# Input rows normed in a layout laid by the host, with mean and deviation spread by one ones matmul a tile in place of eight transposes

## What is computed

```python
def _layernorm(x, axis=-1, eps=1e-05):
    m = jnp.mean(x, axis=axis, keepdims=True)
    v = jnp.var(x, axis=axis, keepdims=True)
    return (x - m) / jnp.sqrt(v + eps)
...
qh = proj(q, Wq, bq)      # q = _layernorm(x): 16 x 128 x 1024, Wq 1024 x 1024
kh = proj(k, Wk, bk)      # k = v = ctx
vh = proj(v, Wv, bv)
qh, kh, vh = (interfere(qh), interfere(kh), interfere(vh))
scores = jnp.einsum('bhqdm,bhkdm->bhqkm', qh, kh) / math.sqrt(dk)
weights = jax.nn.softmax(scores, axis=3)
out = jnp.einsum('bhqkm,bhkdm->bhqdm', weights, vh)
...
x = x + jnp.tanh(g_xattn[0]) * (out @ Wo.T + bo)
x = x + jnp.tanh(g_ffn[0]) * ffn(_layernorm(x))
```

## Time and profile before

| | us |
|---|---|
| three runs | 1361.57, 1362.17, 1358.88 |
| median | 1361.57 |
| the profiled execution: its time | 1363.43 |
| its span in the trace | 1361.1 |
| PE busy in it | 1343.0 (99%) |
| DVE, ACT, POOL busy | 701.5, 409.0, 566.2 |

### The profile page before, as it was taken

One profiled execution on the slowest core, in us unless ns is written; L12 is line 12 of the kernel. 1 busy time (PEld: TensorE's weight loads), 2 busy tenths in 40 slices (PEclk: granted clock), 3 DMA queues, 4 the chain that ended last, 5 costly groups with the idle time before them and its releaser, 6 DMA issues.

```text
span 1361.1 us, 22258 instructions
## 1 busy us (share of the span) xinstructions
PE 1343.0 (99%) x8352; PEld 1116.5 (82%) x8352; DVE 701.5 (52%) x1372; ACT 409.0 (30%) x743; POOL 566.2 (42%) x775
## 2 busy tenths in 40 slices
PE   9999999999999999989999999999999999999999
PEld 8888888888778888778888888888778888888887
DVE  5432433345654545567777777777875243243110
ACT  3312221111112222355555555555451120111100
POOL 0899999999700000445566565655500000000000
PEclk9999999999999999989999999999999999999999
DMA  7898737345347676998877887777442202211011
GB/s 240 247 322 213 193 75 201 139 155 186 124 151 179 163 184 152 261 294 226 229 229 233 229 233 222 220 220 219 173 170 109 78 27 83 78 62 62 32 42 52
DMA packets 188938, 228.16 MB, mean 168 GB/s; under 512 B 26528, under 2 KB 124960, under 8 KB 188832
## 3 DMA queue, kind: packets, MB, share of 16 engines
q1 hardware_dynamic: 162912, 188.46, 46.7%
q10 hardware_dynamic: 25920, 38.28, 9.4%
HBM read 141.74 MB, written 83.89 MB: 166 GB/s over the span
## 4 chain that ended last, share of the span: by engine, by line
PE 69%; POOL 24%; DMA 2%; issue 2%; DVE 1%; ACT 1%; ACTq 1%; SPq 0%; POOLq 0%; DVEq 0%
PE bank L160 13%; PE bank L162 13%; PE bank L161 13%; POOL mixed_part L785 10%; POOL mixed_sum L792 6%; PE bank L1453 5%; PE bank L1473 4%; PE bank L1434 4%; PE bank L1436 4%; PE bank L1488 4%; PE bank L1435 4%; POOL mixed_sum L785 3%; PE bank L349 2%; POOL value_in L792 2%; PE bank L1460 1%
## 5 line engine op out<-in xcount | busy, mean ns | idle before, releaser
L1639 DVE TRANSPOSE_TENSOR_REDUCE part<-bank 128x16 f32<-128x512 f32 x256 | 174.3, 692 | 3.4 <-PE bank L1453 0.8
L1585 ACT ACTIVATE probT<-bank 128x512 f32<-128x512 f32 x256 | 138.9, 595 | 92.8 <-PE bank L1473 89.4
L1434 PE MATMUL bank<-w_hi,oT_hi 128*128 128x512 f32 x256 | 109.3, 427 | 3.3 <-POOL oT_lo L1759 3.0
L1255 DVE SCALAR_TENSOR_TENSOR raw_d<-bank,gates,raw_d 128x512 f32<-128x512 f32 x32 | 24.0, 751 | 167.4 <-PE bank L162 167.4
L160 PE MATMUL bank<-place_b,place_a 128*128 128x512 f32 x256 | 102.2, 399 | 0.4 <-DVE place_c L153 0.4
L160 PE MATMUL bank<-place_a,w_hi 128*128 128x512 f32 x256 | 101.6, 397 | 1.0 <-DVE place_a L153 1.0
L161 PE MATMUL bank<-place_c,place_a 128*128 128x512 f32 x256 | 102.0, 399 | 0.0
L575 DVE SCALAR_TENSOR_TENSOR stage_lo<-bank,bias_mixed,stage_hi 128x512 fp32r<-128x512 f32 x46 | 34.4, 750 | 130.9 <-ACT stage_hi L577 130.9
L160 PE MATMUL bank<-w_hi,yT_hi 128*128 128x512 f32 x256 | 101.8, 398 | 0.0
L1436 PE MATMUL bank<-w_hi,oT_lo 128*128 128x512 f32 x256 | 101.7, 397 | 0.0
L1435 PE MATMUL bank<-w_lo,oT_hi 128*128 128x512 f32 x256 | 101.1, 395 | 0.0
(11 more groups left out here) (241 smaller groups left out, 3076.2 us busy)
## 6 DMA issues: line engine op xcount, KB each, us to landing
k_rows<-stage_hi SPq DMA_DIRECT2D x128, 128.0 KB, 2.6
v_pad<-v_out SPq DMA_DIRECT2D x32, 512.0 KB, 2.6
v_place<-v_pad ACTq DMA_DIRECT2D x64, 256.0 KB, 4.2
tin<-in_ctx_cols SPq DMA_DIRECT2D x26, 512.0 KB, 4.3
k_in<-k_rows SPq DMA_DIRECT2D x64, 192.0 KB, 3.1
q_in<-q_rows SPq DMA_DIRECT2D x128, 96.0 KB, 3.3
q_rows<-wq_own SPq DMA_DIRECT2D x78, 128.0 KB, 2.5
raw_d<-x_mid SPq DMA_DIRECT2D x17, 512.0 KB, 3.3
```

The costliest lines, as they stand in the source:

```text
L1434: pe.matmul(o_bank[out][:], hi[:, c, :], wo_hi[:, k, cols], start=(k == 0), stop=False)
L1585: act.activation(probT[o % NPT][:, i].rearrange("k a p q -> k (a p q)"), two_bank[i][:], ACT.Exp).then_inc(s_exp, 1)
L1639: dve.tensor_reduce(part[o % NS][:, :, 2 * i:2 * i + 2, :].rearrange("k a p b -> k a (p b)"), one_bank[i][:].rearrange("k (a b t) -> k a b ...
```

## The change

The host lays x a second time, as `x_cols`: for each batch, partition p holds column p of each 128-column chunk, all rows (that is x already transposed). Each x tile is loaded twice, as rows (for the statistics) and as columns. `x_norm` still computes mean and inverse deviation from the rows, but writes them as two diagonal 128x128 matrices in place of the normed rows. `x_spread`, a new job, multiplies a 128x128 matrix of ones with the two diagonals side by side (256 columns, plain fp32): every partition of the bank then holds the 128 means and the 128 inverse deviations. Its DVE part subtracts and multiplies the column tile by them, in place. `x_split` adds two jobs without PE work which split the column tile from SBUF. A tile takes three jobs in the line where it took two.

The order moves too. The norm of x tiles 0 to 3 goes from the DVE part of v(8,0) .. v(11,0) to that of v(7,1) .. v(10,1); the PE step of a tile goes from behind v(8,1) .. v(11,1) to between v(8,0) and v(8,1), .. v(11,0) and v(11,1). In the query stage both keep their places. Loads of Wo's rows into `raw1` and `raw2` start later, since the ones, the diagonals and column tiles lie there. The transposes of the second layer stay.

```diff
-                src = ctx_cols[n % NB] if n < CTX else x_t[(n - CTX) * P:(n - CTX + 1) * P, :]
+                src = ctx_cols[n % NB]
...
+            ones = raw[1][:, 0:P]
+            diagonals = [raw[1][:, (1 + 2 * i) * P:(3 + 2 * i) * P] for i in range(2)]
...
+            def load_row_tile(b):
+                slot = b % 2 if b >= GB else 0
...
+                    at = norm_at[b - 1 if b <= GB else b - 2]
+                def load(sp):
+                    if b in (0, GB + 1):
+                        sp.wait_ge(line.emptied, at)
+                    else:
+                        sp.wait_ge(norm.s_stat, b if b <= GB else b - 1)
+                    sp.dma_start(tin[slot], x_t[b * P:(b + 1) * P, :]).then_inc(s_xrow[slot], 16)
...
+            def load_col_tile(b):
+                slot = b % 2 if b < GB else 2 + b % 2
+                tile = (raw[2][:], tin[1], flat_out[0], flat_out[1])[slot]
...
+                    sp.dma_start(tile, x_cols[b]).then_inc(s_xcol[slot], 16)
...
             def x_norm(b, job):
-                n = CTX + b
-                job.dve_pre = norm.vector_steps(b, *load_input(n))
+                tile, landed = load_row_tile(b)
+                norm_at[b] = len(line.jobs)
+
+                def steps(dve):
+                    if b == 0:
+                        link(dve.memset(ones, 1.0))
+                    first_half, variance, inverse, _ = norm.vector_stages(b, tile, landed)
+                    first_half(dve)
+                    variance(dve)
+                    inverse(dve)
+                    link(dve.tensor_scalar(diagonals[b % 2][:, 0:P], ident[:], norm.mv[:, 0:1], None, ALU.mult))
+                    dve.tensor_scalar(diagonals[b % 2][:, P:2 * P], ident[:], norm.rstd[:, 0:1], None,
+                                      ALU.mult).then_inc(norm.s_done, 1)
+                job.dve_pre = steps
                 job.act_pre = norm.scalar_step(b)
-            def x_jobs(b):
-                hi, lo = x_place(b // GB)
-                t_end[CTX + b] = transpose_jobs(line, tin[b % 2], norm.done(b), hi[:, b % GB, :, :], lo[:, b % GB, :, :])
+            def x_spread(b):
+                tile, landed = load_col_tile(b)
+                columns = tile.rearrange("p (k t) -> p k t", t=P)
+                def normalise(bank):
+                    def over_chunks(part):
+                        return bank[:, part * P:(part + 1) * P].unsqueeze(1).to_broadcast([P, KC, P])
+                    link(nc.vector.tensor_tensor(columns, columns, over_chunks(0), ALU.subtract))
+                    return nc.vector.tensor_tensor(columns, columns, over_chunks(1), ALU.mult)
+                spread_end[b] = line.add(Job(
+                    lambda bank: nc.tensor.matmul(bank[:, 0:2 * P], ones, diagonals[b % 2], start=True, stop=True),
+                    normalise, pe_wait=norm.done(b), dve_wait=landed))
+                return tile
+            def x_split(b, tile):
...
+                    def free(act):
+                        if b < GB:
+                            line.wait_filled(act, v_end[VALUE_ORDER[NB - GB + b]])
+                        act.wait_ge(line.emptied, spread_end[b])
+                    t_end[CTX + b] = line.add(Job(
+                        None, lambda bank, lo=lo, hi=hi, cols=cols: split_lo(lo, tile[:, cols], hi),
+                        act=lambda bank, hi=hi, cols=cols: split_hi(hi, tile[:, cols]), act_wait=free))
...
                 v_job(b, 0)
-                if j >= NB - GB:
-                    x_norm(j - NB + GB, line.jobs[-1])
                 if 6 <= j < 6 + KC:
                     query_chunk(j - 6)
+                if j >= NB - GB:
+                    tile = x_spread(j - NB + GB)
                 v_job(b, 1)
+                if NB - GB - 1 <= j < NB - 1:
+                    x_norm(j - NB + GB + 1, line.jobs[-1])
...
-                            x_jobs((g + 1) * GB + (1, 3, 5, 6).index(c))
+                            b = (g + 1) * GB + (1, 3, 5, 6).index(c)
+                            x_split(b, x_spread(b))
```

More of the change, by code:

```diff
@@ L495, in load @@
                 def load(sp):
[L496 to L499, removed]
+                    sp.wait_ge(line.emptied, free)
                     sp.dma_start(tin[slot], src).then_inc(s_tin[slot], 16)
@@ new lines, in build @@
+            diagonals = [raw[1][:, (1 + 2 * i) * P:(3 + 2 * i) * P] for i in range(2)]
+            norm_at, spread_end = {}, {}
+            s_xrow = [sem(f"s_xrow{i}") for i in range(2)]
+            s_xcol = [sem(f"s_xcol{i}") for i in range(4)]
+            def load_row_tile(b):
+                slot = b % 2 if b >= GB else 0
+                use = sum(1 for o in range(b + 1) if (o % 2 if o >= GB else 0) == slot)
+                if b == 0:
+                    at = t_end[CTX - 2]
+                elif b == GB + 1:
+                    at = t_end[CTX + GB - 1]
+                else:
[3 more added lines that the diff above has]
+                        sp.wait_ge(line.emptied, at)
+                    else:
+                        sp.wait_ge(norm.s_stat, b if b <= GB else b - 1)
+                    sp.dma_start(tin[slot], x_t[b * P:(b + 1) * P, :]).then_inc(s_xrow[slot], 16)
+                plan.append((at - 0.5, load))
+                return tin[slot], lambda eng: eng.wait_ge(s_xrow[slot], 16 * use)
@@ new lines, in load_col_tile, with load @@
+            def load_col_tile(b):
+                slot = b % 2 if b < GB else 2 + b % 2
+                use = b // 2 + 1 if b < GB else (b - GB) // 2 + 1
+                tile = (raw[2][:], tin[1], flat_out[0], flat_out[1])[slot]
+                if b in (GB, GB + 1):
+                    at = norm_at[b]
+                elif b == 0:
+                    at = wq_end[4]
+                elif b == 1:
+                    at = t_end[CTX - 1]
+                else:
+                    at = t_end[CTX + b - 2]
+                def load(sp):
+                    if b in (GB, GB + 1):
+                        sp.wait_ge(s_vst[b % 2], 16 * NB)
+                    else:
+                        sp.wait_ge(line.emptied, at)
+                    sp.dma_start(tile, x_cols[b]).then_inc(s_xcol[slot], 16)
+                plan.append((at - 0.4, load))
+                return tile, lambda eng: eng.wait_ge(s_xcol[slot], 16 * use)
@@ new lines, in x_split @@
+            def x_split(b, tile):
+                to_hi, to_lo = x_place(b // GB)
+                for half in range(2):
+                    cols = slice(half * HALF, (half + 1) * HALF)
+                    part = slice(4 * half, 4 * half + 4)
+                    hi = to_hi[:, b % GB, part, :].rearrange("p a b -> p (a b)")
+                    lo = to_lo[:, b % GB, part, :].rearrange("p a b -> p (a b)")
+                    def free(act):
[5 more added lines that the diff above has]
+                        act=lambda bank, hi=hi, cols=cols: split_hi(hi, tile[:, cols]), act_wait=free))
@@ L823, in build @@
                 else:
-                    x_jobs(j - NB + GB)
+                    x_split(j - NB + GB, tile)
+            ring.release(2, t_end[CTX + GB - 2])
             def wo_chunk(c, previous):
@@ L843, in build @@
                         if c in (1, 3, 5, 6):
-                            x_jobs((g + 1) * GB + (1, 3, 5, 6).index(c))
+                            b = (g + 1) * GB + (1, 3, 5, 6).index(c)
+                            x_split(b, x_spread(b))
+                            if b == NB - 1:
+                                ring.release(1, spread_end[b])
                     else:
@@ L851, in zero_queries @@
                         def zero_queries(dve):
-                            line.wait_filled(dve, t_end[CTX + NB - 1])
+                            dve.wait_ge(line.emptied, t_end[CTX + NB - 1])
                             for i in range(2):
@@ L1798 @@
         "x": given["x"],
+        "x_cols": given["x"].reshape(batches, rows, chunks, P).transpose(0, 3, 2, 1).reshape(batches, P, d),
         "ctx_cols": given["ctx_4096"].reshape(batches, rows, chunks, P).transpose(0, 3, 2, 1).reshape(batches, P, d),
```

3 lines of the change are left out of this document (2 added, 1 removed).

## The result

| | before | after |
|---|---|---|
| median, us (6 runs each) | 1361.8 | 1368.34 |
| lowest to highest | 1358.88 to 1362.68 | 1364.94 to 1372.24 |
| profiled execution, its span | 1363.43, 1361.1 | 1367.39, 1365.2 |

The changed kernel is slower: the ratio is 1.0039, with a 95% interval of 1.0021 to 1.0056, which is 5.3 us (2.9 to 7.6). The forecast, 1365.3 us, was 3.0 us too low; the time is inside the range, above the spread given for the likeliest case (1363.3 to 1367.3), and on the slow side of 0.3%, to which the forecast gave 0.45.

What follows compares the result with a forecast made beforehand. PE, busy 99% of the span, was taken to bound the kernel. Value stage +5.5, clock +2.5, query saving -4.9 and borders +0.5 made +3.6, used as +3.7 on 1361.57: 1365.3 us, range 1359.5 to 1370.0.

Steps and rivals of the forecast that it cites:

- the likeliest case: Whole kernel: the sum as worked out, 1365.3 us with a spread of 1363.3 to 1367.3; chance 0.56.
- The wait at tile 2: Value stage: PE idles 7.5 us, 367.15 to 374.7, at tile 2's ones matmul, waiting for DVE behind query weights 7.
- Tile 1: Value stage: PE does not wait for the norm of x tile 1, or 0.5 us at most.
- The ones matmul: PE work added per tile: 0.46 us against 0.87 us of transposes removed, saving 0.41 us a tile.
- the cheap rival: Rival: the ones matmul costs only 0.24 us, 3.1 us less in all, 1362.2 us; chance 0.12.
- The clock: Behind the wait at tile 2 PE's clock falls to its low level, +2.5 us, lost in v(10,1).
- Start of the query stage: q(0,0) starts +5.5 us later from the waits, near 397 in place of 389.0 with the clock's loss.
- The query stage: Twelve tiles save 0.41 us each, -4.9 us; waits of 0.1 to 0.2 us at three group borders give back +0.5.
- The sum: Whole kernel: 5.5 + 2.5 - 4.9 + 0.5 = +3.6 us, taken as +3.7.
- The slow one: Rival: DVE's path is longer at the tight places; 1 us more per product gives 1373 us; 0.18 with the milder one.
- The milder slow one: Rival: PE's pause ahead of q(0,0) brings a second low clock stretch, 1.7 to 2.5 us more, 1367.4; 0.18 with the slower one.
- No wait grows: Rival: no wait grows and all 16 tiles save 0.41 us, -6.6 us, 1355.0 us; chance 0.06.

Runs made afterwards that it cites:

- e1: Changed kernel with the split of query weights 7 moved from between the v jobs of batch 9 to those of batch 10; median 1363.02 us, ratio 1.0003.
- e2: Changed kernel with the ones matmul of x tiles 0 to 2 put back behind both v jobs of its batch; median 1366.87 us, ratio 1.0025.
- e6: Changed kernel with 24 useless matmuls in PE's idle time ahead of its wait at tile 2; median 1370.86 us, ratio 1.0057.
- e4: e1 with the load of column tile 5 moved ahead of the stores of q(0,0) and q(0,1) in SP's list; median 1357.33 us, ratio 0.9967.
- e5: e4 with the query stage's norms and ones matmuls moved so a group's last tile has two q jobs of time; median 1355.56 us, ratio 0.9939.
- e7: e5 with the split of query weights 6 moved later too and six useless matmuls ahead of q(0,0); median 1354.95 us, ratio 0.9936.
- e3: Kernel before the change, with only the split of query weights 7 moved to between the v jobs of batch 10; median 1362.12 us, ratio 0.999.

## Why the prediction was right, and where not

**The wait at tile 2: right.** Its start, its releaser and its cause were as worked out. Counted from V, the ones matmul was forecast at 374.7 - 203.0 = 171.7 us and came at 373.34 - 201.64 = 171.7. The idle time was 6.28 and not 7.5 us, for PE arrived later, first held at tile 1. The products took 1.21 and 1.22 us against 1.2. That the wait comes from the place of query weights 7 is shown by e1; that it is a wait of DVE and not of the moment at which PE asks, by e2.

**Tile 1: too small.** "No wait, 0.5 us at most" was 0.98, 1.40 in the second trace of after and 1.42 in e1. The failed step is the price of the diagonals, 0.23 us each by their columns. Alone they take 0.28, but at 353 us, with POOL mixing, they took 0.61 and 1.31: 1.4 us more. The first part of the norm beside POOL took 3.53 us (349.52 to 353.05) in place of 2.96, another 0.6. The cover was 1.0 us, as forecast, and these 2.0 us used it up and made the wait. The prediction had a row for such contention, and applied it to splits only.

**The ones matmul: right, a little dear.** PE's timeline of after, query stage:

```profile
428.75 0.59 PE L600 MATMUL bank<-raw 128*128 128x256 f32 x2
...
434.67 0.59 PE L600 MATMUL bank<-raw 128*128 128x256 f32 x2
...
442.72 0.51 PE L160 MATMUL bank<-place_b,w_hi 128*128 128x512 f32 x1 [1.95 <-DVE place_b L153]
```

434.67 - 428.75 = 5.92 is a q job of 5.50 and 0.42 for the ones matmul, against the forecast's 0.46 and the cheap rival's 0.24. That rival falls. The saving is 0.45 us a tile and 5.4 us over twelve, against 4.9. The Trainium skill's four passes for true fp32 (FP8 and Floating Point Precision, TensorE Precision Notes) had given an estimate of 0.43; the trace agrees.

**The clock: right in kind, 0.7 too dear.** It fell at tile 2 and was low from 370.3 to 377.1; 3.1 of these 6.8 us lay in PE's idle time. The loss is (386.79 - 373.34) - 0.42 - 2 x 5.63 = 1.8 us, and e6 shows nearly the same, 1.7, by taking it away. The forecast had 2.5.

**Start of the query stage: right, 0.9 too late.** V to Q grew by 7.1 us; the forecast had 5.5 + 2.5 = 8.0. The waits of the stage grew from 2.08 to 9.09 us, the clock took 1.8, and four tiles gave back 1.8.

**The query stage: the mis-sized term.** Forecast -4.9 + 0.5 = -4.4, measured -1.7. The saving was there; the borders took not 0.5 but 3.2 us: 442.72 - 434.67 - 5.92 = 2.13 at q(1,0), and in the same way 0.55 and 0.51 at q(2,0) and q(3,0). Some 0.5 of the stage stay without a place. Two sentences failed. First, "each also takes a place in SP's list, where it waits for the split of the tile before last, long done" is not true of column tile 5, whose load waits for the value stores and stands so far back that it goes out some 16 us later than it can; e4 shows that this was up to 1.7 us. Second, "at tile 7 DVE is free for it" was taken from the row of before, 1.6 us behind PE's request, though DVE gets 2.2 us of work more a tile there. With the load early there are still 0.33 to 0.40 us at each border, and e5, which gives DVE more room, has none. The mean load of DVE in the stage, 99.03 of 145 us, says nothing of this.

**The sum.** The forecast used +3.7, but its terms, unrounded too, add up to +3.6. From V to L +5.4 was measured. The terms miss by +2.7 in the query stage and -0.9 in the value stage; that two misses of opposite sign met in one sum is luck, not part of the account.

**Rivals.** The slow one, DVE late at the tight places, was the right sort with the wrong mechanism: not slower products but a late load and work that came together. The milder slow one, a second fall of the clock ahead of q(0,0), did not occur in either trace of after, but in e1, e4, e5 and e6, after the same pause of 1.82 or 1.83 us; it costs e1 1.7 us. "No wait grows" had -6.6 us. In e7, where hardly a wait is left, V to L is 7.6 us less than before; e3 shows 1.3 of that for the order of query weights 7 alone, which leaves 6.3. So the change is worth about what its arithmetic says once its waits are taken away. That e7's median, 1354.95, is so near that rival's 1355.0 is chance, for before measured 1363.46 beside e7 and not 1361.57.

## To carry to other kernels

Taking work off the busiest engine pays only if the engines that feed it are ready earlier too: before such a change, find each wait with a negative or small margin, and move what stands ahead of the late step (here one split that waits for another engine) out of the list. When a step gains an input, follow that load through the list of its DMA queue to the wait ahead of it; a place that was harmless becomes a bound. When single executions differ by as much as the effect, cut the trace at fixed points and compare the pieces that the edit can reach.

## What the runs showed of the hardware

- Writing a 128x128 diagonal from SBUF takes DVE 0.28 us with POOL idle and 0.61 to 1.40 us beside POOL's `TENSOR_TENSOR` (1.31 at 353.70 above; POOL ran L877 from 353.67 for 1.27). That is up to five times, where a half-tile split went from 0.68 to 1.79. The Trainium skill (GPSIMD Engine Reference, Specifications) says that GpSimd shares its SBUF interfaces with VectorE, with contention for VectorE instructions in a two-port mode or with two SBUF inputs. The longer times agree with sharing; no trace here shows in which mode the diagonal was written.
- A product of a 128x1024 tile with an operand that PSUM repeats eight times costs 1.21 us, no more than a plain split of that size beside it (1.22).
- The clock fell behind a pause of 1.82 or 1.83 us in e1, e4, e5 and e6 and not in two traces of after, whose clock had fallen and returned some 15 us before. Behind the wait of about 2 us at q(1,0) it fell in e2 (2.00) and not in after (1.95), e1 (2.02) and e6 (2.00). In e7 six plain matmuls left 0.44 us of the pause ahead of q(0,0), and the clock stayed at 1.00. The Trainium skill (TensorE: Matmul & The Clock Gate, Why this matters for your kernels) warns of gaps longer than these; by these traces a pause of 1.8 us is enough at times. What tells the cases apart was not settled. A fall behind such a pause cost 1.7 us (e1 against after).
